# Factors of all nodes spread over partitions through DRAM beside other work, in place of products with a matrix of ones, and heavy nodes and row scaling in one stage

## What is computed

```python
def gcn_conv(x, W, b, src, dst, num_nodes):      # used twice; self loops are added to the edges
    h = x @ W
    deg = jax.ops.segment_sum(jnp.ones_like(d, dtype=h.dtype), d, num_segments=num_nodes)
    dinv = jnp.where(deg > 0, jax.lax.rsqrt(deg), 0.0)
    norm = dinv[s] * dinv[d]
    out = jax.ops.segment_sum(h[s] * norm[:, None], d, num_segments=num_nodes)
    return out + b
...
deg = jnp.maximum(jax.ops.segment_sum(jnp.ones_like(dst, dtype=h.dtype), dst, num_segments=n), 1.0)[:, None]
for l in range(n_layers):
    agg = jax.ops.segment_sum(h[src], dst, num_segments=n) / deg
    h = jax.nn.relu(agg @ W_agg[l] + h @ W_self[l] + b_hid[l])
```

## Time and profile before

| | us |
|---|---|
| median of 3 runs (lowest, highest) | 6390.93 (6388.6, 6395.43) |
| profiled execution, device time | 6394.31 |
| its span in the trace | 6392.6 |
| PE busy, share of the span | 4762.7 (75%) |
| DVE busy | 3467.9 (54%) |
| POOL busy | 2448.5 (38%) |
| ACT busy | 1732.2 (27%) |

### The profile page before, as it was taken

How to read it: one execution, slowest core, us unless ns; L and a number is a source line. 1 busy time by engine, 2 the same in 40 slices (tenths; PEclk the granted TensorE clock), 3 DMA queues, 4 the chain that set the end, 5 groups by cost and what they waited for, 6 DMA issues and landing times. The chain is left out here.

```text
span 6392.6 us, 92817 instructions
## 1 busy us (share of the span) xinstructions
PE 4762.7 (75%) x23731; PEld 3336.1 (52%) x23732; DVE 3467.9 (54%) x6884; ACT 1732.2 (27%) x4102; POOL 2448.5 (38%) x2744
## 2 busy tenths in 40 slices
PE   5867879745569976666579789999999494456666
PEld 2213435534347743544456667777777362355545
DVE  8988973656762154999758622231112234555533
ACT  0955643411112243111100333342222221100022
POOL 0847965457418734777300000001111301577500
PEclk9998999855559988888669979999999697776778
DMA  0002437412210067999757100004332321233300
GB/s 30 2 10 111 171 135 233 136 30 35 49 40 15 1 246 293 341 321 321 206 171 236 31 15 10 15 29 126 101 101 77 92 98 51 86 101 102 73 15 20
DMA packets 400513, 683.62 MB, mean 107 GB/s; under 512 B 116655, under 2 KB 286482, under 8 KB 396074
## 3 DMA queue, kind: packets, MB, share of 16 engines
q1 hardware_dynamic: 301826, 425.68, 21.0%
q0 software_dynamic: 98304, 255.53, 13.1%
q10 hardware_dynamic: 192, 0.15, 0.0%
HBM read 448.18 MB, written 232.98 MB: 107 GB/s over the span
## 5 line engine op out<-in xcount | busy, mean ns | idle before, releaser
L3208 POOL CAST sagel_piece<-x 128x1600 fp32r<-128x1600 f16 (+1 forms) x75 | 112.4, 1499 | 1640.3 <-DMA x<-counts 1200.5
L511 POOL DMA_INDIRECT back_sorted<-back_space x391 | 408.4, 1044 | 333.4 <-issue 329.6
L928 POOL DMA_INDIRECT wsum_a_rows<-table,edge_src x416 | 418.0, 1005 | 220.0 <-issue 119.2
L942 PE MATMUL wsum_a_ps<-wsum_a_hot,wsum_a_rows 128*128 128x128 f32 x1664 | 318.0, 369 | 243.6 <-DMA wsum_a_rows<-table,edge_src 141.5
L2047 POOL DMA_INDIRECT big<-hgt_table,edge_key x448 | 424.9, 948 | 181.8 <-issue 110.8
L942 PEld LDWEIGHTS wsum_a_ps<-wsum_a_hot,wsum_a_rows 128*128 128x128 f32 x1664 | 292.1, 272 | 269.5 <-DVE big L969 193.5
L3264 PE MATMUL sagel_ps<-sagel_piece,sagel_high 128*128 128x512 f32 (+1 forms) x1050 | 399.4, 388 | 0.8 <-issue 0.8
L511 POOL DMA_INDIRECT own_sorted<-big x256 | 286.8, 1120 | 294.8 <-issue 293.8
L3264 PE MATMUL sagel_ps<-sagel_piece,sagel_low 128*128 128x512 f32 (+1 forms) x1050 | 379.9, 375 | 0.0
L2095 PE MATMUL hgt_s_pq<-big 128*128 x1344 | 246.7, 348 | 177.1 <-DVE hgt_s_tmp L2134 153.5
L716 PE MATMUL cnt_ps<-cnt_hot_s,cnt_hot_d 128*128 128x512 bf16 (+1 forms) x1792 | 324.6, 335 | 67.1 <-DVE cnt_hot_s L698 58.3
(11 more groups left out here) (989 smaller groups left out, 10970.0 us busy)
## 6 DMA issues: line engine op xcount, KB each, us to landing
hgt_edge_values<-big SPq DMA_DIRECT2D x112, 512.0 KB
big<-hgt_edge_values SPq DMA_DIRECT2D x112, 512.0 KB, 4.4
x<-counts SPq DMA_DIRECT2D x75, 400.0 KB, 3.1
x<-counts SPq DMA_DIRECT2D x75, 384.0 KB, 3.1
counts<-big SPq DMA_DIRECT2D x25, 832.0 KB
counts<-big SPq DMA_DIRECT2D x25, 768.0 KB
big<-counts SPq DMA_DIRECT2D x30, 640.0 KB, 5.8
counts_turned<-big SPq DMA_DIRECT2D x30, 640.0 KB, 3.9
```

The source lines that it names most:

```text
L511: self.nc.gpsimd.indirect_dma_start(self.e.dram, bass.IndirectOffsetOnAxis(ap=self.adr[:, c:c + 1], axis=0), self.rec[:, c, :], None).then ...
L928: nc.gpsimd.indirect_dma_start(rows[n % DEEP][:, u, :], None, table, bass.IndirectOffsetOnAxis(ap=e.src[:, g:g + 1], axis=0)).then_inc(gat ...
L942: mm = nc.tensor.matmul(ps[r.slot % 2][u][:, k * P:(k + 1) * P], rows[r.slot][:, u, k * P:(k + 1) * P], hot[r.slot % 2][:, u, :], start=Tr ...
```

## The change

Both uses of `rows_to_all` go. In each, the [128, 25] factors are turned to [25, 128] by one transpose, copied to SBUF by ACT, stored as 3200 floats in DRAM (12.5 KB), and read back by one DMA with a partition step of zero, so that each of 128 partitions receives the whole row (1600 KB). For the convolution all of it lies in gcn_a1: TensorE's first instruction there is the transpose, ACT's first is the copy, SP issues the store behind its four first fetches, waits for it and issues the read; DVE waits for the read ahead of the first `scale`. For the graph layer the factors are made and stored in soft_bn, and the read joins the loads beside the layer norm of `sage_stage`, as the fifth of 14; `sage_v0` goes. The stages `heavy_nodes` and `gcn_scale` become one.

```diff
-def gcn_scale(nc, kit, g):
...
-    rows_to_all(nc, kit, "gcn_dall", g.dinv, g.dall)
...
                     for k in range(RING):
                         fetch(k)
+
+                    sp.wait_ge(row_out, 1)
+                    sp.dma_start(dinv_dram.rearrange("(t p) -> t p", p=P), dinv_row[:]).then_inc(row_stored, 16)
+                    sp.wait_ge(row_stored, 16)
+                    sp.dma_start(dall, row_to_all(dinv_dram)).then_inc(row_back, 16)
                     for q in range(len(loads)):
...
+                    nc.tensor.transpose(px[0:NT, 0:P], dinv[:], kit.ident[:]).then_inc(row_turned, 1)
                     pe.wait_ge(made, 1)
...
                         if i == SPARE_TURN:
                             pe.wait_ge(spare_out, 1)
+                            pe.wait_ge(row_out, 1)
...
+                    act.wait_ge(row_turned, 1)
+                    nc.scalar.copy(dinv_row[:], px[0:NT, 0:P]).then_inc(row_out, 1)
                     first_part(0)
...
                         dve.wait_ge(summed, w + 1)
+                        if w == 0:
+                            dve.wait_ge(row_back, 16)
...
+                @block.tensor
+                def _(pe):
+                    pe.wait_ge(shared, 2)
+                    nc.tensor.transpose(ps[0:NT, 0:P], rdeg[:], kit.ident[:]).then_inc(row_turned, 1)
+
+                @block.sync
+                def _(sp):
+                    sp.wait_ge(row_out, 1)
+                    sp.dma_start(rdeg_dram.rearrange("(t p) -> t p", p=P), rdeg_row[:]).then_inc(row_stored, 16)
+                    sp.wait_ge(row_stored, 16)
+
                 @block.vector
                 def _(dve):
+                    nc.vector.tensor_scalar(rdeg[:], kit.deg_out[:], 1.0, None, ALU.max).then_inc(shared, 1)
+                    dve.wait_ge(shared, 1)
+                    nc.vector.reciprocal(rdeg[:], rdeg[:]).then_inc(shared, 1)
                     link = link_on(dve, step)
...
+                    act.wait_ge(row_turned, 1)
+                    nc.scalar.copy(rdeg_row[:], ps[0:NT, 0:P]).then_inc(row_out, 1)
...
-def heavy_nodes(nc, kit):
+def scale_and_heavy_nodes(nc, kit, g):
...
+                nc.vector.tensor_scalar(g.dinv[:], kit.deg_in[:], 1.0, None, ALU.add).then_inc(grown, 1)
                 link(nc.vector.tensor_scalar(flag[:], kit.deg_in[:], float(EXACT), None, ALU.is_gt))
                 link(nc.vector.memset(zeros[:], 0.0))
                 link(nc.vector.tensor_copy(node[:, :, 0], kit.node[:]))
                 link(nc.vector.memset(node[:, :, 1], 1.0))
+                dve.wait_ge(rooted, 1)
+                nc.vector.reciprocal(g.dinv[:], g.dinv[:]).then_inc(scaled, 1)
+                dve.wait_ge(scaled, 1)
+                nc.vector.tensor_tensor(g.rows, g.rows, per_node(g.dinv[:], P), ALU.mult).then_inc(scaled, 1)
                 dve.wait_ge(ranked, 1)
...
+                dve.wait_ge(scaled, 2)
+
+            @block.scalar
+            def _(act):
+                act.wait_ge(grown, 1)
+                nc.scalar.activation(g.dinv[:], g.dinv[:], ACT.Sqrt).then_inc(rooted, 1)
...
-                            (bias_in[:], column(A["L2_gnn_b_in"], 2)), (bias_out[:], row_to_all(A["L2_gnn_b_out"]))]
+                            (bias_in[:], column(A["L2_gnn_b_in"], 2)), (bias_out[:], row_to_all(A["L2_gnn_b_out"])),
+                            (rall[:], row_to_all(rdeg_dram))]
...
-        def mean_factor(link):
-            link(nc.vector.tensor_scalar(rdeg[:], kit.deg_out[:], 1.0, None, ALU.max))
-            link(nc.vector.reciprocal(rdeg[:], rdeg[:]))
-        on_vector(nc, "sage_v0", mean_factor)
-        rows_to_all(nc, kit, "sage_rall", rdeg, rall)
...
-                    heavy_nodes(nc, kit)
-                    gcn_scale(nc, kit, g)
+                    scale_and_heavy_nodes(nc, kit, g)
```

More of the change, by code:

```diff
@@ L1186, in gcn_first @@
     return g
-def gcn_scale(nc, kit, g):
-    with ExitStack() as cc:
-        step, rooted = sems(nc, cc, "gcn_dinv", "step rooted")
-        with nc.Block() as block:
-            @block.vector
-            def _(dve):
-                nc.vector.tensor_scalar(g.dinv[:], kit.deg_in[:], 1.0, None, ALU.add).then_inc(step, 1)
-                dve.wait_ge(rooted, 1)
-                nc.vector.reciprocal(g.dinv[:], g.dinv[:]).then_inc(step, 1)
-                dve.wait_ge(step, 2)
-                nc.vector.tensor_tensor(g.rows, g.rows, per_node(g.dinv[:], P), ALU.mult).then_inc(step, 1)
-                dve.wait_ge(step, 3)
-            @block.scalar
-            def _(act):
-                act.wait_ge(step, 1)
-                nc.scalar.activation(g.dinv[:], g.dinv[:], ACT.Sqrt).then_inc(rooted, 1)
-    rows_to_all(nc, kit, "gcn_dall", g.dinv, g.dall)
 def gcn_stage(nc, kit, g, x, bufs, counts, counts16, counts_t, beside1, beside2):
@@ L1267, in gcn_stage @@
             stored = gather_sems(nc, "gcn_a1", "stored", 2)
+            row_turned, row_out = sems(nc, c, "gcn_row", "row_turned row_out")
+            (row_stored,), (row_back,) = (gather_sems(nc, "gcn_row", n, 1) for n in ("stored", "back"))
+            dinv_row = c.enter_context(nc.sbuf_tensor("gcn_dinv_row", [NT, P], F32))
+            dinv_dram = nc.dram_tensor("dinv_row", (NP,), F32).ap()
             put_spare, spare_rows = heavy_rows(nc, c, kit, counts, counts16, big1)
@@ L1811, in columns, with soft_moe_stage @@
     return ap2d.rearrange("e (k p) -> p (e k)", p=P)
-def soft_moe_stage(nc, kit, A, x, bufs):
+def soft_moe_stage(nc, kit, A, x, bufs, rdeg_dram):
     b2 = bufs[1]
@@ L1833, in soft_moe_stage @@
         with ExitStack() as cc:
-            step, rooted = sems(nc, cc, "soft_bn", "step rooted")
-            with nc.Block() as block:
+            step, rooted, shared, row_turned, row_out = sems(nc, cc, "soft_bn", "step rooted shared row_turned row_out")
+            row_stored, = gather_sems(nc, "soft_bn", "row_stored", 1)
+            rdeg = cc.enter_context(nc.sbuf_tensor("soft_rdeg", [P, NT], F32))
+            rdeg_row = cc.enter_context(nc.sbuf_tensor("soft_rdeg_row", [NT, P], F32))
+            ps = cc.enter_context(nc.psum_tensor("soft_rdeg_ps", [P, 512], F32))
+            with nc.Block() as block:
+                @block.tensor
[7 more added lines that the diff above has]
+                    sp.wait_ge(row_stored, 16)
                 @block.vector
                 def _(dve):
+                    nc.vector.tensor_scalar(rdeg[:], kit.deg_out[:], 1.0, None, ALU.max).then_inc(shared, 1)
+                    dve.wait_ge(shared, 1)
+                    nc.vector.reciprocal(rdeg[:], rdeg[:]).then_inc(shared, 1)
                     link = link_on(dve, step)
@@ L3070, in heavy_nodes @@
         ps = [c.enter_context(nc.psum_tensor(f"heavy_ps{n}", [P, 512], F32)) for n in range(2)]
-        step, ranked, picked = sems(nc, c, "heavy", "step ranked picked")
+        step, grown, rooted, scaled, ranked, picked = sems(nc, c, "heavy", "step grown rooted scaled ranked picked")
         with nc.Block() as block:
@@ L3130, in heavy_rows, with sage_stage @@
     return on_pool, stored
-def sage_stage(nc, kit, A, x, b3, b4, counts16):
+def sage_stage(nc, kit, A, x, b3, b4, counts16, rdeg_dram):
     with ExitStack() as c:
@@ L3143, in sage_stage @@
         bias = [sb(f"b_hid{i}", [P, 2]) for i in range(layers)]
-        rdeg, rall = sb("rdeg", [P, NT]), sb("rall", [P, NP])
+        rall = sb("rall", [P, NP])
         with ExitStack() as cc, nc.allow_non_contiguous_dma(reason="short bias columns"):
@@ L3800, in program @@
         counts16 = nc.dram_tensor("counts16", (NP, NP), F16).ap()
+        rdeg_dram = nc.dram_tensor("rdeg_row", (NP,), F32).ap()
         counts_t = nc.dram_tensor("counts_turned", (NP, NP), F16).ap()
@@ L3846, in program @@
             hgt_stage(nc, kit, A, x, bufs, edges, order)
-            soft_moe_stage(nc, kit, A, x, bufs)
-        sage_stage(nc, kit, A, x, big3, big4, counts16)
+            soft_moe_stage(nc, kit, A, x, bufs, rdeg_dram)
+        sage_stage(nc, kit, A, x, big3, big4, counts16, rdeg_dram)
         back_sort.fetch()
```

## The result

The changed kernel takes **6370.07 us** (median of 7 runs, 6366.82 to 6378.56), the kernel before 6390.93 (7 runs, 6387.76 to 6397.67). The ratio is 0.997, interval 0.996 to 0.9979. Predicted were 6373.0 and a range of 6364 to 6381. Of the 26 executions of the kernel before in that second set, one took 6743.11 us at a lower granted clock and is left out of the ratios.

What follows compares the result with a forecast made beforehand. No engine was taken to bound the whole; stages parted by barriers count in full. The terms -11.8 + 1.4 - 9.25 + 1.7 = -17.95 from 6390.93 gave 6373.0 us, range 6364 to 6381.

Steps and rivals of the forecast that it cites:

- Heavy nodes and scaling, -11.8: From the degrees to gcn_a1: it starts 11.8 us sooner, some 10 from dropping rows_to_all, 1.8 from the merge.
- gcn_a1, nothing: In gcn_a1: the row's transpose, copy, store and read cost nothing, up to 2 us if the read meets fetches later.
- so it has at least 14 us of slack: In gcn_a1: the fifth fetch, delayed behind the row's read, is not needed for at least 14 us.
- Rival A: In gcn_a1: DVE starts ahead of POOL, so DVE's stall shrinks, gaining 5 of 10 us, giving 6368; chance 0.12.
- soft_bn, +1.4: From soft_bn to the gates: making and storing the row delays the gates by 1.4 us, bounds +0.5 to +3.2.
- 2.8 from issue to landing: In soft_bn: SP's store of the row takes 2.8 us, as a small DMA alone, and ends the stage.
- The graph layer, -9.25: From norm to projection: the projection starts 9.25 us sooner, the last load ending the stage; bounds -6.65 to -10.9.
- the read at 412 GB/s, 4.0 us: In the graph layer's loads: the 1.64 MB row read runs at another layer's broadcast rate and adds 4.0 us.
- The clock, +1.7: In the graph layer's projection: 3.4 us at TensorE's 1.2 GHz fall on it and cost 1.7 us.
- Rival C: Both row reads: one DRAM row read by 16 DMA engines is far slower, a loss from 18.0 us; chance 0.03.
- Rival B: Whole change: covers are thin, broadcast at 248 GB/s, late store, 2 us in gcn_a1, giving 6379.8; chance 0.12 with D.
- D: Both rows_to_all: the loop goes but its time stays, as gcn_a1 or projection waits for something hidden; chance within Rival B's 0.12.

Runs made afterwards that it cites:

- second set: Later executions made with the follow-up experiments: the kernel before has a median of 6396.19 us (26 runs), the control 6382.65 us (10 runs).
- e_row_twice: Changed kernel, with SP reading the scaling row twice in gcn_a1 and waiting for each read before the stores; 6380.22 us, one execution.
- control: Changed kernel with only a register maximum with zero ahead of waits on loaded values, as in all experiments; median 6382.65 us (10 runs), ratio 0.9981.
- e_gcn_only: Changed kernel with the graph layer and soft_bn as before, so only the convolution's part of the change; median 6384.34 us (10 runs), ratio 0.9982.
- e_rall_late: Changed kernel with the graph layer's row read beside the projection, behind the store of x, not beside the norm; median 6375.31 us (5 runs), ratio 0.9966.
- e_rall_last: Changed kernel with the degrees' row read as the last of the graph layer's loads, not the fifth; 6373.9 us, one execution.
- e_busy: Changed kernel with 16 more unread float32 products on TensorE behind the last transposes of the graph layer's norm; 6382.13 us, one execution.
- e_rall_alone: Changed kernel with the degrees' row read in a stage of its own between the graph layer's norm and projection; 6375.52 us, one execution.
- e_merge_only: Kernel before with only the joint stage for heavy nodes and scaling, both rows_to_all kept; median 6397.74 us (10 runs), ratio 1.0.
- e_before_pool: Kernel before, with POOL's cast and subtraction of heavy rows in gcn_a1 waiting for DVE's subtractions and one-hots; 6384.87 us, one execution.
- e_pool_late: Changed kernel, with POOL's cast and subtraction of heavy rows in gcn_a1 waiting for DVE's subtractions and one-hots; median 6370.66 us, ratio 0.9972.

## Why the prediction was right, point by point

- **Heavy nodes and scaling, -11.8.** Measured 13.20 - 25.15 = -11.95. The boundary was 0.50 as taken, and the split (10 for `rows_to_all`, 1.8 for the merge) came out as 10.4 and 1.54. (The bound of -12.1 should read -12.0: 931.8 + 0.28 against 944.1.)
- **gcn_a1, nothing.** Measured 173.78 - 174.93 = -1.15, within the stage's scatter, and DVE's 6.85 was still there. The price was right, its reason partly wrong, and this part is luck. The step "so it has at least 14 us of slack" looked at the fifth fetch. The store of the row landed 12.21 after the first fetch, where 954 had meant 9.9, and the read took 7.4 from issue to landing. What SP's wait and the read threaten is the first store of turned blocks, for which the third block's copies wait. Slack there is 2.7 us, up to 5 at most (`e_row_twice`), and the row is free only under POOL's stall; without it, it costs 6.4 (169.91 against 163.46).
- **Rival A.** It did not decide the profiled run of the changed kernel, but it is real, and its chance was too low: of seven profiles with this gcn_a1 and POOL not held back (changed, control, `e_gcn_only`, `e_rall_late`, `e_rall_last`, `e_busy`, `e_rall_alone`), two have DVE's third part and remainder both held (173.78 and 176.44) and five a shorter stall (169.37 to 172.06). The means of the two groups are 4.5 apart, changed and control 4.4, where I had 5. Both profiles with the old gcn_a1 and POOL not held back (before, `e_merge_only`) have the full stall. So over executions the stage gained more than the nothing that I put down; how often in the changed kernel itself is open, since one execution of it was profiled. The Trainium skill, "SBUF — State Buffer", section "Who interferes with whom", has GpSimd and VectorE share an exclusive lock. The traces agree: DVE's held operation ends 0.68 us after POOL's (951.91 and 951.23), and none is held in `e_before_pool`.
- **soft_bn, +1.4.** Measured +0.36, under the lower bound of 0.5. The step that failed is "2.8 from issue to landing": the store took 2.0 or less and hid behind DVE's chain. The 2.8 was that of a load issued third in a row, 0.9 us behind the first, and so not of a DMA alone.
- **The graph layer, -9.25.** Measured 17.02 - 24.85 = -7.83. The mis-sized term is the read at 412 GB/s, 4.0 us. The last bytes came about 15.2 after the norm's start, before 9.7: 5.6 us for 1.64 MB, 294 GB/s. Three rows bear on it: beside the weights the DMA engines together ran at 363 to 395 GB/s; alone the read takes 3 us to come to 410; and the last biases were issued up to 4279.4, 11.6 after the norm's start, since SP's issues took up to 4.52 for three, which left a tail of 0.12 MB from 4281.5 to 4283.0. `e_rall_last` puts the biases' part at about 0.7 to 1.2; the rest is not split by any run. The Trainium skill's 358 GB/s ("SBUF — State Buffer", section "A bandwidth-pool intuition that's wrong"), by which I had an estimate of 4.6, was nearer to this stretch than my 412, though windows of 410 to 422 (`e_rall_alone`) stand against it as a ceiling.
- **The clock, +1.7.** Measured +2.89. The cause was right (`e_busy` takes it away), the duration was one of two: 3.4 us in the old trace, 6.8 in this one, of which 5.9 fell on the projection. Had it been 3.4 again, the cost would have been about the 1.5 to 1.7 of `e_pool_late`, `e_row_twice` and `e_rall_last`.
- **The sum.** The five touched stretches give -11.95 - 1.15 + 0.36 - 7.83 + 2.89 = -17.68, against -17.95 predicted: the layer's 2.6 too much were given back by 1.0 in soft_bn and 1.15 in gcn_a1. That the errors cancel to 0.3 is luck. The profiled runs lie 24.2 apart, so 6.6 of that is in stages with the same code, which differ as much between other profiles (the stretch of the switch layer took 433.8 to 441.2). That the median came to 2.9 us below the forecast is no more than this scatter, with rival A as a possible part; in the control's set the same change gave 13.5, 4.4 less than forecast.
- **Rival C** is out (7.0 us and not 18). **Rival B** was half right, for the graph layer only, and **D** likewise: 3.1 of the 11 us of the second `rows_to_all` stayed as a wait for the loads, and 2.9 came back through the clock. `e_rall_late` wins both, by its stretches.

## What to carry to other kernels

A transfer moved "beside other work" is free only if every transfer queued behind it has slack as well: look at the store with the fewest buffers, not at the next fetch. A cost of nothing may hang on another fault (here the stall of 11.5 us behind POOL); remove that and the cost appears. And a stage that ends on a DMA while TensorE idles can pay twice, the wait and then the lower clock.

## What the runs showed of the hardware that was not expected

- Two engines' elementwise work in SBUF held each other up: DVE's 0.82 us became 6.85 beside POOL's 6.69, and POOL's cast of 2.84 us took 2.95 to 3.45 where DVE had started first. The order of two starts, which turned by 1.4 us between runs of the same code, decided over 4.4 us of the stage. DVE's copies out of PSUM beside POOL's subtraction took their usual 0.4 us (two in 0.74, control).
- Pauses of TensorE of 3.6 to 8.0 us were followed by 1.2 GHz for either 3.4 or 6.8 us, pauses of 2.55 to 2.85 by 3.4 us or by none, pauses of about 1.2 by none.
- A read of one 12.5 KB row to 128 partitions alone in the queues needs 3 us to come to its full 410 GB/s, 7.0 in all. The same bytes in seven pieces between other transfers cost gcn_a1 2.0 us (165.41 against 163.46), in one piece 6.5 (169.98).
